# Attention on one core: value products of four key tiles in one TensorE visit, and the first row-sum part one step earlier

## What is computed

```
qkv = einsum('bnc,dc->bnd', layernorm(x), qkv_w) + qkv_b
attn = einsum('bhqd,bhkd->bhqk', q, k) * scale
attn = softmax(attn, axis=-1)
out = einsum('bhqk,bhkd->bhqd', attn, v)
y = einsum('bnc,dc->bnd', out, proj_w) + proj_b
result = x + y + expert_ffn(layernorm(x))
```

## Time and profile before

| | us |
|---|---|
| median of three runs | 4841.46 (4841.42 to 4845.11) |
| the profiled execution, its own time | 4836.55 |
| span of the profile | 4834.7 |
| TensorE busy | 4691.4 (97%) |
| TensorE weight loads busy | 2773.0 (57%) |
| VectorE busy | 3170.4 (66%) |
| ScalarE busy | 2398.9 (50%) |
| GpSimd busy | 3223.0 (67%) |

### The profile page before, as it was taken

One profiled execution on the slowest core, in us unless ns is written; L12 is line 12 of the kernel. 1 busy time (PEld: TensorE's weight loads), 2 busy tenths in 40 slices (PEclk: granted clock), 3 DMA queues, 4 the chain that ended last, 5 costly groups with the idle time before them and its releaser, 6 DMA issues. The chain is left out here.

```text
span 4834.7 us, 66456 instructions
## 1 busy us (share of the span) xinstructions
PE 4691.4 (97%) x24396; PEld 2773.0 (57%) x24396; DVE 3170.4 (66%) x5296; ACT 2398.9 (50%) x4653; POOL 3223.0 (67%) x1117
## 2 busy tenths in 40 slices
PE   8999999999899999999999999999999999999979
PEld 6887878878654444444444444444444444444447
DVE  4223232333188888888888888888888888888534
ACT  2111121121146666666666666666666666666621
POOL 1121212121249998989989989999899998998920
PEclk9999999999979999999999999999999999999989
DMA  5344343343346655656656566665665656655466
GB/s 172 103 127 122 109 138 102 119 129 111 91 106 130 137 127 125 138 125 137 133 124 139 124 131 136 126 139 120 132 137 124 140 125 132 137 124 121 90 225 236
DMA packets 254215, 633.49 MB, mean 131 GB/s; under 512 B 45252, under 2 KB 79044, under 8 KB 212936
## 3 DMA queue, kind: packets, MB, share of 16 engines
q0 software_dynamic: 36864, 268.45, 27.8%
q1 hardware_dynamic: 217032, 360.85, 27.0%
HBM read 224.96 MB, written 134.74 MB: 74 GB/s over the span
## 5 line engine op out<-in xcount | busy, mean ns | idle before, releaser
L927 DVE TENSOR_REDUCE unit_max<-mx_ps 128x1 f32<-128x512 f32 x4096 | 2535.2, 681 | 317.0 <-PE mx_ps L1002 310.9
L836 POOL TENSOR_TENSOR p_pair<-p_sb 128x2048 f32<-128x2048 f32 x512 | 2439.8, 4811 | 185.3 <-PE mx_ps L1026 128.3
L913 ACT ACTIVATE p_sb<-st_ps 128x512 f32<-128x512 f32 x4096 | 2061.9, 628 | 905.5 <-PE st_ps L1073 905.5
L1002 PE MATMUL mx_ps<-k_x,q_x 96*128 96x512 f32 x4096 | 1684.9, 415 | 21.5 <-DMA k_x<-k_lo_d 19.6
L1073 PE MATMUL st_ps<-q_x,k_x 97*128 97x512 f32 x4096 | 1607.8, 413 | 37.9 <-ACT p_sb L913 37.3
L1073 PEld LDWEIGHTS st_ps<-q_x,k_x 97*128 97x128 f32 x4096 | 770.3, 188 | 599.3 <-ACT p_sb L913 512.8
L1002 PEld LDWEIGHTS mx_ps<-k_x,q_x 96*128 96x128 f32 x4096 | 784.6, 192 | 456.7 <-DVE unit_max L927 234.3
L1014 PE MATMUL o_ps<-p_sb,v_sb 128*32 128x512 f32 x8192 | 986.8, 599 | 0.0
L285 POOL TENSOR_TENSOR h_lo<-h_f,h_hi 128x512 fp32r<-128x512 f32 x128 | 165.2, 1291 | 687.7 <-DVE h_hi L469 687.7
L1014 PEld LDWEIGHTS o_ps<-p_sb,v_sb 128*32 128x32 f32 x8192 | 214.0, 109 | 494.1 <-ACT p_sb L913 309.8
L469 DVE CAST h_hi<-h_f 128x512 fp32r<-128x512 f32 x128 | 55.0, 431 | 541.9 <-ACT h_f L342 541.9
(11 more groups left out here) (94 smaller groups left out, 3926.8 us busy)
## 6 DMA issues: line engine op xcount, KB each, us to landing
p_pair<-p_pair POOLq DMA_DIRECT2D x256, 1024.0 KB, 7.3
q_x<-q_hi_d SPq DMA_DIRECT2D x128, 256.0 KB, 8.6
k_x<-k_hi_d SPq DMA_DIRECT2D x68, 256.0 KB, 7.3
xt<-x SPq DMA_DIRECT2D x64, 256.0 KB, 2.7
stage<-w SPq DMA_DIRECT2D x32, 512.0 KB, 5.1
q_hi_d<-qk_hi SPq DMA_DIRECT2D x64, 256.0 KB, 3.0
q_lo_d<-qk_lo SPq DMA_DIRECT2D x64, 256.0 KB, 3.9
k_hi_d<-qk_hi SPq DMA_DIRECT2D x64, 256.0 KB, 2.6
```

Source lines behind the costliest of these rows:

```text
L836: pool.tensor_tensor(p_pair[:, slot, :, :], p_sb[:, n % SLOTS, :, :], p_sb[:, (n + 1) % SLOTS, :, :], ALU.add).then_inc(pair_done, 1)
L913: act.activation(p_sb[:, (L * G * KT + n) % SLOTS, h, :], st_ps[bank(g, m)][:, :], ACT.Exp, scale=SCALE).then_inc(exp_done, 1)
L927: dve.reduce_max(unit_max[:, n // 4, n % 4:n % 4 + 1], mx_ps[UNIT_PLACE[n] % RING][:, :], AX.X).then_inc(bank_read, 1)
L1002: pe.matmul(mx_ps[UNIT_PLACE[n] % RING][:, :], q_x[qc][0:R, h, t * P:(t + 1) * P], k_x[u][0:R, h, kc * 512:(kc + 1) * 512], start=True, st ...
```

## The change

The value products of four key tiles are done together, at the steps 0, 2, 4 and 6 of a group; the steps 1, 3, 5 and 7 have no `V`. At step j the tiles 2j-4 to 2j-1 are done (at j=0 the last four of the group before), and the first wait of a group for `v_sb` and for the copied `o_ps` moves from j=1 to j=2. The first row-sum part moves from step 7 to step 6, where it stands behind the transpose (`VTZ`). The third part stays at step 3, which has no `V` any more, so it is a visit of its own. The end of the stage does four key tiles where it did two.

```diff
--- before.py
+++ after.py
@@ -600,7 +600,7 @@
 
 
     NA, NJ = NP + 1, 4
-    PARTS = [(2, 0, False, 7), (4, 0, True, 10), (0, NA, False, 11)]
+    PARTS = [(2, 0, False, 6), (4, 0, True, 10), (0, NA, False, 11)]
     NS = len(PARTS)
     ctx = ExitStack()
     with ctx:
@@ -650,8 +650,8 @@
 
 
 
-        STEPS = ["USUSUSUVUSSUSUSUS", "USUSUSUVUSSUSUSUS", "USUSUSUVZUSSUSUSUS", "USUSUSUVZUSSUSUSUS",
-                 "USUSUSUVUSSUSUSUS", "USUSUSUVUSSUSUSUS", "USUSUSUVTUSSUSUSUS", "USUSUSUVZUSSUSUSUS"]
+        STEPS = ["USUSUSUVUSSUSUSUS", "USUSUSUUSSUSUSUS", "USUSUSUVZUSSUSUSUS", "USUSUSUZUSSUSUSUS",
+                 "USUSUSUVUSSUSUSUS", "USUSUSUUSSUSUSUS", "USUSUSUVTZUSSUSUSUS", "USUSUSUUSSUSUSUS"]
         FIRST = sum(s.count("U") for s in STEPS[AHEAD:])
         PARTS_AT = [at for _, _, _, at in PARTS]
 
@@ -1077,14 +1077,14 @@
 
                             if j == 0:
                                 if not (first and g == 0):
-                                    for kt in (KT - 2, KT - 1):
+                                    for kt in range(KT - 4, KT):
                                         values(L, (g - 1) * KT + kt, (g - 1) % G // QC, kt)
                                 return
-                            if j == 1:
+                            if j == 2:
                                 pe.wait_ge(v_ld[u], (L + 1) * 16)
                                 if not (first and g == 0):
                                     pe.wait_ge(o_copied, L * G + g)
-                            for kt in (2 * j - 2, 2 * j - 1):
+                            for kt in range(2 * j - 4, 2 * j):
                                 values(L, g * KT + kt, u, kt)
 
                         def sum_parts(j, place):
```

## The result

The change makes the kernel slightly slower. The median of 17 runs is 4853.86 us (4850.48 to 4859.09), against 4844.38 us (4838.56 to 4848.75) of before in 17 runs beside them. The ratio is 1.002, 95% interval 1.0013 to 1.0028, so +9.5 us. That is inside the range given, but on the other side of nothing from the forecast (-6 us). The profiled execution has a span of 4852.8 us.

A forecast was written before the change was run, and what follows sets the result against it. TensorE's group period of 50.65 us was taken as the bound: stretches, visits and a ScalarE wait. Stretches 24.20 + 7.46, visits 18.64 and transpose 0.25 gave 50.55; over about 62 groups -6 us, median 4835 us, range 4825 to 4852.

The forecast's parts named there:

- the long stretches: Three runs of 16 units between visits: 24.20 us a group where six stretches took 22.38, so 1.82 us more.
- VectorE's ring: Four banks that VectorE's maxima free at 0.598 us each; unit 16 waits for unit 12's bank in 16-unit stretches.
- the short ones: The two stretches of 8 units around the part alone at step 3: 3.73 us each, 7.46 together.
- The wait of ScalarE: A score waits for ScalarE, whose copy waits for GpSimd's normalisation; forecast to go, 0.79 us a group less.
- The part alone at step 3: Step 3's visit with only a row-sum part and no value products: 1.32 us.
- the plain visit of step 4: Four key tiles of value products without a row-sum part: 3.90 us.
- The first rival: In long stretches the ring never binds and ScalarE sets the pace: 49.21 us a group, 4752 us; chance 0.10.
- the second: The ScalarE wait stays because normalisation waits for the inverse sums: 51.34 us a group, 4884 us; chance 0.17.
- the third: The row-sum part at step 6 waits for its join, 1 us late: about 4897 us; chance 0.05.
- The visits: Five visits a group, 3.90 us plain and 4.76 with a row-sum part: 18.64 us against 20.02, so 1.38 less.
- The transpose: At step 6, between value products and row-sum part: 0.25 us more a group; 0.39 if mode changes drain TensorE.
- three terms of 0.8 to 1.8 us: Per group: visits -1.38 us, longer stretches +1.82, ScalarE wait -0.79.

The follow-up runs named there:

- e4: The changed kernel with unit maxima over 256 of 512 columns, exponential's scale divided by 8: 4742.29 us, ratio to before 0.9794.
- e9: The kernel before with the first row-sum part at step 6, ahead of the transpose, and maxima over 256 of 512 columns: 4771.66 us, ratio 0.9859.
- e1: The kernel before with only the first row-sum part moved to step 6, ahead of the transpose: 4793.44 us, ratio to before 0.9901.
- e2: The kernel before with the first row-sum part moved to step 6, behind the transpose: 4812.36 us, ratio to before 0.9937.
- e3: The changed kernel with the row-sum part ahead of the transpose at step 6 (VZT for VTZ): 4830.27 us, ratio to before 0.9973.

## Why the forecast missed

**What held.** In the group from 2401.97 to 2452.77 the long stretches measured 7.96, 8.07 and 8.05 us, 24.08 in all for the 24.20 forecast; the short ones 3.72 and 3.73 for 3.73. VectorE's ring sets the long ones, as e4 and e9 show. The wait of ScalarE went (0.79 forecast, 0.76 in e1). The part alone at step 3 took 1.31 us for 1.32, the plain visit of step 4 3.89 for 3.90. The first rival, that the ring might not bind, didn't come; neither did the second nor the third: no copy waited for GpSimd, and step 6 waited for no join.

**What failed** are two terms of the sum. The visits: 3.90 and 4.76 us were read off visits whose last unit was on time. Three of the five now stand behind a late unit, with weights that aren't loaded ahead, and cost 0.10 us more each (4.00, 4.86, and that much of 5.21). I had allowed for the delay between VectorE's read and the unit, and not for what follows the unit. The transpose: 0.25 us, ends 0.15 and 0.44, measured 0.35 by e2 against e1 and by the change against e3. In the rows it is 0.11 more going in, as forecast, and 0.21 going out for the 0.14 taken; the rest is a row-sum part that takes 0.02 to 0.03 us longer.

Together they turn 50.55 into 50.80: +0.30 and +0.10 for the two terms, -0.12 for the long stretches, -0.03 for the rest. The forecast of -0.10 us a group was a balance of three terms of 0.8 to 1.8 us, so +0.25 is enough to change its sign. The first term is a cost that the sum put at nothing, and the range had no end for it either; that 50.80 still lies under the range's upper end of 50.83 is in part luck, since that end was made of a dearer transpose and a slower release of the ring alone.

The 0.21 us between transpose and row-sum part is less than the transpose's shown 0.28, so these rows don't show a wait for its whole duration. By the drain rule of TensorEngine Tiling in the Trainium skill (Key Properties), as the prediction worked it out, the transpose would have cost an estimated 0.39 us. The measured 0.35 is nearer to that than to my 0.25.

**Where the expected gain went**, by edit, in us a group: moving the part -0.76 (e1), merging the visits +0.57 (e3 against e1), the transpose's place +0.35 (the change against e3, and the same by e2 against e1). The sum is +0.15 before rounding, as measured. Of the merging, the visits gave back 1.1 us (20.02 to 18.92 without the transpose's 0.35) and the stretches took 1.7 (29.84 to 31.53).

## What to carry to other kernels

A stretch between two switches of the array can be as long as the slowest reader of its ring allows: multiply out when unit n+4 needs the bank of unit n, and end the stretch before. When the order of a ring's writer is full to that point, count the instruction behind a late one as dearer too: here it started 0.10 us later. Keep whole-array work like a transpose at the edge of a run of 32-column work, and try each part of a bundled change alone: here one of three edits gave all the gain. And see what holds a control up before you read it: one whose period is set by another loop can't show that an edit brings nothing.

## What was not expected of the hardware

A unit that waits for its bank is shown with 0.50 us for 0.40, its weight load starts with it and not 0.12 us ahead, and the next instruction starts 0.34 us (score) or 0.43 us (value product) behind it, where it is 0.23 and 0.33 otherwise. So such a wait ahead of a visit costs 0.10 us beyond itself; inside a stretch that goes at VectorE's pace of 0.60 us it isn't seen.

TensorE's busy share rose from 395.6 to 399.9 of 400 us while the kernel became slower. Its meaning shows beside e1 (the same window), and in a wait of before from 2000 to 4000 us:

```profile
2400.00:2800.00 400.00, 399.67 (x2257) 197.03 (x2260) 334.29 (x554) 265.48 (x530) 367.95 (x114) 1.00 0.63 133
```

```profile
PE st_ps L1073 <- ACT p_sb L913: 21.3, 39, 0.9
```

The wait of a score for ScalarE was nearly all of TensorE's idle time before: 0.55 us a group, 4.3 us in 400. It is gone in e1, where TensorE is as full and the kernel 49 us faster than before, and in the change, where it is 9.5 us slower. The new waits leave no gap in the rows. Late units are 0.60 us apart, a score starts 0.34 us behind one and is shown 0.40 long, and the next unit starts 0.26 us behind the score. So the share tells neither the gain nor the loss; the period of the groups does.
